# A four-layer decoder kernel: in its attention stages the raw exponentials are weighed with the values, and the reciprocals of the row sums are turned and multiplied into the heads

## The reference

```python
qh = (layernorm(x) @ w_q.T + b_q) ...                 # 16 heads of 8
attn = softmax(einsum('bhtd,bhsd->bhts', qh, kh) * 8 ** -0.5, axis=-1)
ctx = einsum('bhts,bhsd->bhtd', attn, vh)             # heads side by side: 128 features
out = ctx @ out_w.T + out_b
x = x + tanh(g_xattn[layer]) * out
```

## Time and profile before

| | |
|---|---|
| median device time of three runs | 1531.48 us |
| span of the profiled execution, first to last instruction | 1500.5 us |
| what lies around the span, as median less span | 31.0 us |
| attention `l1x`: subtraction of the maximum, first to last start | 219.9 to 361.3 us |
| the same in `l2x` | 715.8 to 856.9 us |
| the same in `l3x` | 984.6 to 1132.4 us |
| mean granted TensorE clock | 0.888 of full speed |

### The profile page before, as it was taken

One profiled execution on the slowest core, in us unless ns is written; L12 is line 12 of the kernel. 1 busy time (PEld: TensorE's weight loads), 2 busy tenths in 40 slices (PEclk: granted clock), 3 DMA queues, 4 the chain that ended last, 5 costly groups with the idle time before them and its releaser, 6 DMA issues. The chain is left out here.

```text
span 1500.5 us, 24814 instructions
## 1 busy us (share of the span) xinstructions
PE 1159.1 (77%) x8806; PEld 806.5 (54%) x8806; DVE 975.4 (65%) x1859; ACT 769.5 (51%) x1393; POOL 941.7 (63%) x1085
## 2 busy tenths in 40 slices
PE   5672578999429999564688868769997886999983
PEld 5331455565328998264355535635555553766552
DVE  6789859997361211354899958869994586544421
ACT  3487356777435454264577756537775441222220
POOL 5200048998326553584799979559997252788885
PEclk9795798999659999787799979979997796999997
DMA  3000001110037887111111000011110213444442
GB/s 110 8 0 0 0 23 30 36 36 18 4 113 208 245 228 194 50 51 30 52 36 35 19 17 1 0 36 36 36 36 2 81 43 100 88 103 98 97 75 25
DMA packets 62157, 89.96 MB, mean 60 GB/s; under 512 B 10378, under 2 KB 33684, under 8 KB 61780
## 3 DMA queue, kind: packets, MB, share of 16 engines
q1 hardware_dynamic: 46228, 70.14, 15.0%
q0 software_dynamic: 15808, 18.24, 7.3%
HBM read 57.03 MB, written 16.12 MB: 49 GB/s over the span
## 5 line engine op out<-in xcount | busy, mean ns | idle before, releaser
L1653 PE MATMUL ps<-topk_up_sb,topk_wu 128*128 128x512 f32 x256 | 121.0, 616 | 0.7 <-issue 0.7
L1555 ACT ACTIVATE topk_ga<-ps 128x512 f32<-128x512 f32 x64 | 38.2, 598 | 158.0 <-PE ps L1653 158.0
L147 POOL TENSOR_SCALAR sb_stage<-sb_x,l0f_rstd,l0f_shift 128x128 f32<-128x128 f32 x48 | 24.5, 526 | 146.6 <-DVE l0f_shift L134 146.3
L1476 POOL DMA_INDIRECT out<-topk_shared,l3f_route_slots x64 | 103.0, 1609 | 20.4 <-issue 14.6
L2162 DVE TENSOR_TENSOR l1f_g_y<-ps,l1f_g_wd 128x256 f32<-128x256 f32 x39 | 16.6, 425 | 134.3 <-PE ps L2105 134.3
L1794 DVE TENSOR_TENSOR sb_xnT<-topk_ga,ps 128x512 f32<-128x512 f32 x64 | 43.9, 686 | 87.1 <-ACT topk_ga L1555 87.1
L2132 ACT ACTIVATE l1f_g_h<-ps,l1f_g_wd 128x256 f32<-128x256 f32 x156 | 63.0, 475 | 72.4 <-DMA l1f_g_wd<-l1f_W 40.4
L1472 POOL DMA_INDIRECT topk_xg<-l3f_rows,l3f_route_slots x64 | 77.8, 1215 | 19.7 <-issue 17.7
L2044 POOL DMA_INDIRECT l1f_g_xg<-l1f_rows,l1f_route_slots x78 | 74.9, 961 | 17.7 <-issue 12.5
L537 POOL TENSOR_TENSOR l1x_prob<-l1x_prob,l1x_rden 128x1232 f32<-128x1232 f32 x32 | 72.0, 2249 | 14.3 <-DVE l1x_rden L706 14.3
L537 POOL TENSOR_TENSOR l2x_prob<-l2x_prob,l2x_rden 128x1232 f32<-128x1232 f32 x32 | 72.0, 2250 | 13.9 <-DVE l2x_rden L706 13.9
(11 more groups left out here) (507 smaller groups left out, 3529.4 us busy)
## 6 DMA issues: line engine op xcount, KB each, us to landing
l1f_g_wd<-l1f_W SPq DMA_DIRECT2D x39, 322.0 KB, 4.0
l1f_g_wu<-l1f_W SPq DMA_DIRECT2D x39, 256.0 KB, 3.7
topk_wu<-l3f_W SPq DMA_DIRECT2D x16, 512.0 KB, 3.6
l1f_y_rows<-l1f_g_y SPq DMA_DIRECT2D x39, 128.0 KB, 3.9
topk_wd<-l3f_W SPq DMA_DIRECT2D x16, 256.0 KB, 3.0
l1x_vrows<-sb_l0f_up SPq DMA_DIRECT2D x16, 154.0 KB
l2x_vrows<-l2x_vall SPq DMA_DIRECT2D x16, 154.0 KB
l3x_vrows<-l3x_vall SPq DMA_DIRECT2D x16, 154.0 KB
```

The source lines that it names most:

```text
L1476: pool.indirect_dma_start(out=out_rows, out_offset=spot(g, i), in_=y[g % 2][:, i, :], in_offset=None, compute_op=ALU.add).then_inc(y_added ...
L1653: ins = pe.matmul(ps[:, 2 * (c % 2) + i, :], wu[g % W][:, (i * CX + c) * P:(i * CX + c + 1) * P], xgT[g % 2][:], start=True, stop=True)
```

## The change

All of it is in `attention`. The weights are no longer divided. `turn` takes the raw exponentials, and `weigh` makes unnormalised heads. Beside this, POOL adds the two halves of each row of 77 (`fold`: 16x38 sums and a copy of the odd column, into `half`), and DVE sums over 39 in place of 77 (`total`). The 16 reciprocals of a token are spread to 128 columns by ACT (`widen`), turned by PE (`turn_share`), copied out of PSUM by ACT together with the heads (`keep_heads`, 256 columns), and multiplied into the heads by POOL (`heads`). The output bias goes through a product on PE in both stages that have it, with the bias of v folded into it once (`ROW`), so `bias` on POOL is gone. `AHEAD` is 2. The three turned pieces have PSUM banks 0, 1 and 6 of their own; heads, turned reciprocals and output share bank 7.

```diff
-    AHEAD = 4
+    AHEAD = 2
+    H = KEYS // 2 + 1
+    TURN = (0, 1, 6)
...
-            def divide(n):
-                pool.wait_ge(recip, n + 1)
-                pool.tensor_tensor(prob[n % 4][:], prob[n % 4][:], rden[n % 2][:].unsqueeze(2).broadcast_to([P, HEADS, KEYS]), ALU.mult).then_inc(normed, 1)
...
+            def fold(n):
+                pool.wait_ge(exped, n + 1)
+                if n >= 2:
+                    pool.wait_ge(summed, n - 1)
+                pool.tensor_tensor(half[n % 2][:, :, 0:H - 1], prob[n % 4][:, :, 0:H - 1], prob[n % 4][:, :, H - 1:KEYS - 1], ALU.add).then_inc(folded, 1)
+                pool.tensor_copy(half[n % 2][:, :, H - 1:H], prob[n % 4][:, :, KEYS - 1:KEYS]).then_inc(folded, 1)
+
+            def heads(n):
+                pool.wait_ge(both_kept, n + 1)
+                if n >= 2:
+                    pool.wait_ge(out_made, n - 1)
+                pool.tensor_tensor(oT[n % 2][:], both[n % 2][:, 0:P], both[n % 2][:, P:2 * P], ALU.mult).then_inc(heads_kept, 1)
...
-            for it in range(1 - AHEAD, NT):
-                if it + AHEAD + 1 < NT:
-                    keys(it + AHEAD + 1)
-                if 0 <= it + 1 < NT:
-                    values(it + 1)
-                if it >= 1:
-                    add(it - 1)
-                if masked and it >= 0:
-                    bias(it)
-                if 0 <= it + AHEAD - 2 < NT:
-                    divide(it + AHEAD - 2)
-            add(NT - 1)
+            keys(2)
+            for k in range(NT + 2):
+                if k + 3 < NT:
+                    keys(k + 3)
+                if k >= 2:
+                    add(k - 2)
+                if k < NT:
+                    fold(k)
+                if 1 <= k <= NT:
+                    heads(k - 1)
+                if k < NT:
+                    values(k)
...
+            def turn_share(n):
+                pe.wait_ge(widened, n + 1)
+                pe.transpose(SHARE, wide[n % 2][:].rearrange("p h d -> p (h d)"), t["ident"][:]).then_inc(share_turned, 1)
+
+            def weigh(n):
+                pe.wait_ge(vpad_ready, n + 1)
+                if n >= 1:
+                    pe.wait_ge(both_kept, n)
+                if n >= 2:
+                    pe.wait_ge(out_kept, n - 1)
...
+            for k in range(NT + 2):
+                if 1 <= k <= NT:
+                    weigh(k - 1)
+                if k >= 2:
+                    output(k - 2)
+                if 1 <= k <= NT:
+                    turn_share(k - 1)
+                if k < NT:
+                    turn(k)
+                if k + AHEAD < NT:
+                    score(k + AHEAD)
...
+            def widen(n):
+                sc.wait_ge(recip, n + 1)
+                if n >= 2:
+                    sc.wait_ge(share_turned, n - 1)
+                sc.activation(wide[n % 2][:], rden[n % 2][:].unsqueeze(2).broadcast_to([P, HEADS, HD]), ACT.Copy).then_inc(widened, 1)
+
+            def keep_heads(n):
+                sc.wait_ge(heads_made, n + 1)
+                sc.wait_ge(share_turned, n + 1)
+                if n >= 2:
+                    sc.wait_ge(heads_kept, n - 1)
+                sc.activation(both[n % 2][:], OT_SHARE, ACT.Copy).then_inc(both_kept, 1)
...
+            exponent(0)
+            for k in range(NT + 2):
+                if 1 <= k <= NT:
+                    widen(k - 1)
+                    keep_heads(k - 1)
+                if k >= 2:
+                    keep_out(k - 2)
+                if k < NT:
+                    keep_turned(k)
+                if k + 1 < NT:
+                    exponent(k + 1)
...
             def total(n):
-                v.wait_ge(exped, n + 1)
-                v.tensor_reduce(rowsum[n % 2][:], prob[n % 4][:], X, ALU.add).then_inc(summed, 1)
+                v.wait_ge(folded, 2 * (n + 1))
+                v.tensor_reduce(rowsum[n % 2][:], half[n % 2][:], X, ALU.add).then_inc(summed, 1)
...
+            for k in range(NT + 2):
+                if k + 1 < NT:
+                    largest(k + 1)
+                    shift(k + 1)
+                if k >= 2:
+                    spread(k - 2)
+                if k < NT:
+                    total(k)
+                if k >= 2:
+                    joined(k - 2)
+                if k < NT:
+                    invert(k)
```

More of the change, by code:

```diff
@@ L606, in weigh, with turn @@
-            def weigh(n, c):
-                if c == 0:
-                    pe.wait_ge(vpad_ready, n + 1)
-                    if n >= 1:
-                        pe.wait_ge(heads_kept, n)
-                pe.wait_ge(turned_kept, PIECES * n + c + 1)
-                rows = min(L, GK - L * c)
-                for g in range(GROUPS):
-                    ins = pe.matmul(ps[32 * g:32 * g + 32, 0, 0:P], vpad[n % 2][0:rows, c, 32 * g:32 * g + 32], pt[n % 2][0:rows, c, g, :],
-                                    start=(c == 0), stop=(c == PIECES - 1), tile_position=(0, 32 * g))
-                if c == PIECES - 1:
-                    ins.then_inc(heads_made, 1)
+            def turn(n):
+                pe.wait_ge(exped, n + 1)
+                weights = prob[n % 4][:].rearrange("p h k -> p (h k)")
+                for c in range(PIECES):
+                    if n >= 1:
+                        pe.wait_ge(turned_kept, PIECES * (n - 1) + c + 1)
+                    for g in range(GROUPS):
+                        at = piece(g, c)
+                        ins = pe.transpose(ps[0:at.stop - at.start, TURN[c], g * P:g * P + P], weights[:, at], t["ident"][:])
+                    ins.then_inc(turned, 1)
@@ new lines, in turn_share @@
+            def turn_share(n):
[7 more added lines that the diff above has]
+                    pe.wait_ge(out_kept, n - 1)
+                if n == 0 and bias_out:
+                    pe.wait_ge(row_ready, 1)
+                for c in range(PIECES):
+                    pe.wait_ge(turned_kept, PIECES * n + c + 1)
+                    rows = min(L, GK - L * c)
+                    for g in range(GROUPS):
+                        ins = pe.matmul(ps[32 * g:32 * g + 32, 7, 0:P], vpad[n % 2][0:rows, c, 32 * g:32 * g + 32], pt[n % 2][0:rows, c, g, :],
+                                        start=(c == 0), stop=(c == PIECES - 1), tile_position=(0, 32 * g))
+                ins.then_inc(heads_made, 1)
@@ L716, in joined @@
                 v.bn_aggr(t["mv"][:, n, :], st[:, n % 2, :]).then_inc(var_ready, 1)
-            for n in range(AHEAD - 1):
-                largest(n)
-                shift(n)
-                if n >= 1:
-                    total(n - 1)
-                    invert(n - 1)
-            for n in range(NT):
-                ahead, behind = n + AHEAD - 1, n - 2
-                if ahead < NT:
-                    largest(ahead)
-                if behind >= 0:
-                    spread(behind)
-                if ahead < NT:
-                    shift(ahead)
-                if ahead - 1 < NT:
-                    total(ahead - 1)
-                if behind >= 0:
-                    joined(behind)
-                if ahead - 1 < NT:
-                    invert(ahead - 1)
-            for n in range(NT - 2, NT):
-                spread(n)
-                joined(n)
+            largest(0)
+            shift(0)
+            if bias_out:
+                v.wait_ge(loads, 16)
+                if bias_v:
+                    v.wait_ge(row_made, 1)
+                    v.tensor_tensor(bo[:], bo[:], ROW, ALU.add).then_inc(row_ready, 1)
+                else:
+                    v.tensor_copy(bo[:], bo[:]).then_inc(row_ready, 1)
+            for k in range(NT + 2):
[10 more added lines that the diff above has]
+                    invert(k)
 def quantised_ffn(nc, t, d, gate_at, later):
```

97 lines of the change are left out of this document (24 added, 73 removed).

## The result

| | before | changed |
|---|---|---|
| median device time | 1532.96 us (1530.89 to 1534.96, 4 runs) | 1648.51 us (1644.98 to 1652.04, 4 runs) |
| ratio, 95% interval | | 1.0748 (1.0726 to 1.0770) |
| span of the profiled execution | 1500.5 us | 1647.1 us |
| from first to last subtraction, three stages | 141.4, 141.1, 147.8 us | 186.5, 172.0, 181.5 us |
| from there to the start of the last variance | 17.0, 14.9, 15.3 us | 18.4, 15.5, 19.4 us |

The kernel is slower, by 115.6 us.

The account below looks back on a forecast made before the run. The prediction took a ring of waits to set the pace: +57.8, +45.6 and +52.5 us over three stages, +3 for stage ends (+159), +25 for the clock: +184 on 1531.5, 1715 us, range 1650 to 1785.

Parts of the forecast that it names:

- The ring: Loop of waits keep_out, add, fold, heads, values, weigh, output, turn_share, keep_heads: 6.49 us a tile, 6.07 second stage; chance 0.82.
- the forecast's signs: Expected in the profile after: POOL waiting before addition, PE before `weigh`, subtractions 6.5 us apart, fold 1.4 to 1.5.
- The rival of the engines' sums: POOL and PE never wait for each other; the longest engine sets 4.2, 4.1, 4.85 us a tile: 1510 us; chance 0.04.
- The terms: Prices of one round's steps, among them fold 1.45, `weigh` 1.0, `output` 0.84, `turn_share` 0.42; sum 6.49 us.
- Not all ends meet: Reason for the range 1650 to 1785 us, though unknown terms allowed -56 to +33 us and the clock -25 to +40.
- The rule against the fold: Skill's 2.6 cycles an element for two inputs on GpSimd, sending elementwise work to VectorE; estimated 1.5 us for the fold.
- First steps: Only the first step of each stage stays as it is; 30 steps at the new pace follow.
- Ends of stages: From last subtraction to last variance: 17.2 us before, 18.1 after, +1 a stage, +3 in all.
- The clock: PE's idle gap lowers its granted clock now and then, +1.5 us a tile in a quarter of early-stage tiles: +25 us.
- The rival that it stays down: Each round's gap keeps PE's clock at half, all 93 steps pay 1.5 us: 1830 us; chance 0.08.
- 31.0 us around the span: Time taken to lie outside the profiled execution; the forecast added +184 to the median 1531.5 us, with a span of 1684.5.

Follow-up runs that it names:

- run 4: Changed kernel plus an unused second product of the keys on POOL behind the fold's copy, ahead of the values: 1693.93 us, 1.1271.
- run 3: Changed kernel plus an unused second product of the keys on POOL behind `keys`, where POOL waits next: 1622.88 us, 1.0793.
- run 1: Changed kernel with POOL issuing the values of a tile one tile earlier, ahead of the addition into x: 1516.24 us, 1.0061.
- run 2: Changed kernel with POOL issuing the fold ahead of the addition into x, not behind it: 1480.20 us, 0.9836.
- run 9: Changed kernel with POOL's order keys, fold, addition into x, heads, values of the next tile: 1496.32 us, 0.9758.
- run 6: Changed kernel plus eight GpSimd test instructions on spare buffers, three times each, at the head of the first attention stage: 1689.93 us, one run, not compared.
- run 5: Changed kernel plus eight unread transposes of the identity on TensorE per tile, ahead of the wait for the values: 1631.70 us, 1.0651.

## Why the prediction was right in kind and wrong in size

**The ring: right, and shown.** Both waits stand in the trace, work put in the ring lengthens a round by its own time, 5.87 to 6.53 in the first stage (run 4), the same work beside it does not (run 3), and taking `values` or the fold off it gives nearly all of the loss back or more (runs 1 and 2). The scores two tiles ahead, which every run keeps, are not the cause. Of the forecast's signs the waits and the clock came as named (POOL idle only ahead of the addition, PE idle 2.02 us ahead of `weigh`, 0.82 and 0.88); the distance of 6.5 us, the fold of 1.4 to 1.5 and DVE busy under two thirds (it was 69 to 75%) did not. The rival of the engines' sums, 4.1 a tile, is not what this order does, but it is what run 9 reaches: the edge that had to get slack was the order on POOL.

**The terms: the failed step.** The forecast's round was 6.49, the measured one 5.87. The difference is in three terms. The fold was taken at 1.45 and took 1.21: its rate was set by "two full inputs", and the form of the fold, with its second input 38 elements behind the first, is cheaper (run 6). `weigh` was taken at 1.0 and took 0.80: its 24 products stand in one record of 0.87, 0.27 a piece, where the earlier trace rows had pieces between other products at 0.35. And `output` with `turn_share` took 1.10 (0.41 + 0.33 + 0.36) in place of 1.26. That is 0.24 + 0.20 + 0.16, and 0.02 in the small ones, 0.62 together. By 30 rounds in each stage it makes 55.5 us of the 68 that are missing.

**"Not all ends meet": wrong.** The low ends of the terms make the round 0.6 shorter, -56 us, and those of the clock -25; together they reach down to 1634 us, and the range began at 1650. But the terms were priced from instructions in other surroundings (another distance of inputs, another neighbour), and all fell low together: the fold to 1.21, near its low end of 1.16 (the 1.20 less the overlap), `weigh` to 0.80, below its 0.90, and `output`, which had no low end, to 0.74 from 0.84. With both low ends in full the range would have held the time.

**The rule against the fold.** The forecast worked out 1.5 and 2.9 us by the Trainium skill's 2.6 cycles an element ("GPSIMD Engine Reference", section "Elementwise — side-by-side cycle accounting"). By that rate alone the estimates are 1.32 us for 608 elements and 2.67 for 1232; the rest is the fixed 0.18 of the rows. The fold's record took 1.27, the division's 2.25.

**First steps: too long by 9.** At full clock (run 5) the three stages have 521.3 us between the subtractions; 30 measured rounds in each and the forecast's first steps make 530.8. The ring is not full at the head of a stage: the first four steps of the first stage are 4.53, 3.92, 3.92 and 5.51, where the forecast had only the first one faster. In the same way the kernel before has four steps of 5.6 to 5.7 us at the head of its third stage, not one, and a steady step of 4.63, where the forecast read 4.74.

**Ends of stages: +6 where +3 was forecast.** Two thirds of it is the third stage, 19.4 against 15.3 us. At full clock (run 5) the ends are 16.9, 14.9 and 16.9, so all but 1.5 us of the +6 is the clock. The forecast took the end of before from the first stage alone.

**The clock: 19 us between the subtractions where 25 was forecast.** "Now and then" was right: the windows show 0.82, 0.88 and 0.92. `weigh` at three of four tiles in a row of the changed kernel (the one at 310.80 stands above), and the granted clock (column before the last two) of the windows between them:

```profile
304.94 0.87 PE L621 MATMUL ps<-l1x_pt,l1x_vpad 103*32 103x128 f32 x24 [0.75 <-POOL l1x_vpad L534]
...
316.67 1.06 PE L621 MATMUL ps<-l1x_pt,l1x_vpad 103*32 103x128 f32 x24 [2.02 <-POOL l1x_vpad L534]
...
323.46 1.12 PE L621 MATMUL ps<-l1x_pt,l1x_vpad 103*32 103x128 f32 x24 [0.16 <-POOL l1x_vpad L534]
```

```profile
310.80:316.60 5.80, 3.85 (x49) 2.86 (x49) 4.11 (x7) 3.46 (x8) 3.79 (x7) 1.00 0.00 0
316.60:323.00 6.40, 6.33 (x49) 4.76 (x49) 3.80 (x6) 3.04 (x7) 3.49 (x7) 0.55 0.32 94
323.00:329.00 6.00, 4.39 (x53) 3.08 (x49) 4.20 (x6) 4.12 (x8) 3.78 (x7) 0.91 0.02 8
```

Together with the 2.02 us ahead of 310.80 above, two gaps of the same length stood there: the first was followed by a round at 1.00, the second by one at 0.55, the level of 1.2 GHz, which took 6.79 us. That round left a gap of 0.16, and the clock came back. The rival that it stays down (1830 us) is refuted. The Trainium skill ("TensorE: Matmul & The Clock Gate", section "HAM oscillation — how this bites in real kernels") describes a loop that restarts cold in every round; its recurring wait, some 3 to 5 us, is longer than the gap here, and no run here has so long a gap in each round. In this trace gaps of 2.02 us were enough to be followed by the lower level in some rounds, and that the slow round fills its own gap is the likely reason why it did not stay.

**The addition of the parts:** -55.5 (terms), -9 (first steps), -6 (clock), +3 (ends) make -67.5 from +184, and +116 was measured.

**"31.0 us around the span": misread.** It was the difference between a profiled execution and the median of others, most likely on a slower chip: in every later run 1.7 us lie around the span. It did not move the forecast, which added a difference to the median, but spans of two kernels are not to be compared here.

## What to carry to other kernels

Before an instruction is moved on an in-order queue, follow the waits from it over the other engines until they come back; if they come back one tile later, the sum round the ring is the pace, however idle each engine is. Cheaper work beside the ring gains nothing then, and a change of place in the queue does: with the same instructions on each engine the five orders span 0.9758 to 1.0748. Where the terms of such a sum are priced from rows in another surrounding, let the range reach the corner where all miss to the same side, since the number of rounds multiplies them together.

## What the runs showed of the hardware that I had not expected

- The cost of a two-input instruction on GpSimd depends on where the inputs lie: 608 elements take 1265 ns in 16 rows with the second input 38 elements behind the first, 1488 in such rows from two tiles, and 1462 in one piece, 608 apart or from two tiles (run 6). The Trainium skill ("GPSIMD Engine Reference", section "Elementwise — side-by-side cycle accounting") has one rate for two inputs, 2.6 cycles, an estimate of 1.3 us for 608 elements with no fixed cost; it does not tell these rows apart.
- With VectorE busy or idle the fold takes the same: in run 2 its 96 records last 1265 to 1285 ns, the three with VectorE idle throughout 1272 to 1276, and the ten with VectorE busy throughout 1265 to 1276.
- A piece of `weigh` on TensorE took 0.35 us between products of another kind, and 0.27 where three pieces follow each other.
- After gaps of 2.0 us the granted clock fell in some rounds and not in others; with eight idle transpositions in them it stayed at 0.99 (run 5).
- The same gather of rows took 89 to 93 us on one chip and 107 to 111 on two others.
